# A layered graph kernel: the target column goes through DRAM, and the score addition moves from TensorE and VectorE to GpSimd and ScalarE

## The reference, cut to what matters

```
s, t = h @ u_s, h @ u_t                  # 512-long dot products, one pair per node
e    = leaky_relu(s[:, None] + t[None, :] (+ bias in L2))
e    = where(edge, e, -1e9 or -inf)
out  = softmax(e, axis=-1) @ h           # L0 then applies elu, which changes nothing here
```

## Time and profile before

| | |
|---|---|
| median of 3 runs | 3774.3 us (3770.13 to 3774.59) |
| the profiled execution | 3771.3 us |
| its span, first to last instruction | 3769.4 us |
| granted TensorE clock, mean | 0.986 |
| VectorE, ScalarE, GpSimd busy, share of the span | 82%, 52%, 50% |

### The profile page before, as it was taken

How to read it: one execution, slowest core, us unless ns; L and a number is a source line. 1 busy time by engine, 2 the same in 40 slices (tenths; PEclk the granted TensorE clock), 3 DMA queues, 4 the chain that set the end, 5 groups by cost and what they waited for, 6 DMA issues and landing times.

```text
span 3769.4 us, 75317 instructions
## 1 busy us (share of the span) xinstructions
PE 3567.6 (95%) x25488; PEld 3231.1 (86%) x25488; DVE 3088.7 (82%) x6892; ACT 1949.1 (52%) x4770; POOL 1867.9 (50%) x2852
## 2 busy tenths in 40 slices
PE   3899999999999999999999999999999999999996
PEld 2788888888888888888888888888888888888885
DVE  6788888888888888888888888888888888888874
ACT  2455555555555555555555555555555555555552
POOL 4355455445455545555554554554555545545543
PEclk7999999999999999999999999999999999999997
DMA  3000000000000000000000000000000000000000
GB/s 122 14 20 20 26 20 20 26 20 20 23 23 20 20 26 20 20 26 20 20 26 20 20 26 20 20 26 20 20 26 20 20 26 20 20 23 23 20 16 12
DMA packets 62512, 90.10 MB, mean 24 GB/s; under 512 B 9265, under 2 KB 25777, under 8 KB 62129
## 3 DMA queue, kind: packets, MB, share of 16 engines
q1 hardware_dynamic: 62128, 85.30, 6.9%
HBM read 51.72 MB, written 33.55 MB: 23 GB/s over the span
## 4 chain that ended last, share of the span: by engine, by line
PE 73%; DVE 16%; ACT 5%; issue 4%; POOL 1%; DVEq 0%; ACTq 0%; POOLq 0%
PE bank_c L360 20%; PE bank_b L360 18%; PE bank_e L360 10%; PE bank_e L401 6%; DVE product L805 5%; PE bank_a L368 4%; PE bank_e L380 4%; PE bank_e L335 3%; PE bank_b L335 3%; DVE g L1045 2%; DVE x L831 2%; DVE nlE L1016 2%; DVE nlE L1028 2%; ACT g_hi L740 2%; ACT xa L702 2%
## 5 line engine op out<-in xcount | busy, mean ns | idle before, releaser
L598 ACT ACTIVATE h<-x,rs 128x512 f32<-128x512 f32 x384 | 311.8, 812 | 383.5 <-POOL rs L1114 383.5
L360 PE MATMUL bank_c<-w_hi,g_hi 128*128 128x258 f32 x2048 | 433.2, 293 | 76.4 <-ACT g_hi L740 75.7
L1109 POOL TENSOR_SCALAR rs<-mv 128x1 f32<-128x1 f32 x512 | 142.0, 277 | 688.3 <-DVE mv L798 659.4
L1189 POOL TENSOR_TENSOR nlE<-nlE,nmE 128x512 f32<-128x512 f32 x256 | 265.9, 1038 | 416.1 <-DVE nmE L1036 416.1
L360 PE MATMUL bank_c<-w_lo,g_hi 128*128 128x258 f32 x2048 | 413.3, 283 | 0.0
L360 PE MATMUL bank_b<-w_lo,hT_hi 128*128 128x344 f32 x1536 | 409.3, 321 | 0.0
L360 PE MATMUL bank_b<-w_hi,hT_hi 128*128 128x344 f32 x1536 | 408.7, 320 | 0.0
L360 PEld LDWEIGHTS bank_c<-w_hi,g_hi 128*128 128x128 f32 x2048 | 314.8, 189 | 97.4 <-ACT g_hi L740 96.4
L360 PE MATMUL bank_c<-w_hi,g_lo 128*128 128x258 f32 x2048 | 350.7, 283 | 0.0
L360 PE MATMUL bank_b<-w_hi,hT_lo 128*128 128x344 f32 x1536 | 345.8, 320 | 0.0
L656 ACT ACTIVATE hT_hi<-bank_e 128x512 fp32r<-128x512 f32 x128 | 76.7, 600 | 499.6 <-PE bank_e L352 499.6
(11 more groups left out here) (158 smaller groups left out, 10294.7 us busy)
## 6 DMA issues: line engine op xcount, KB each, us to landing
x_in<-in_x SPq DMA_DIRECT2D x128, 256.0 KB, 2.6
out<-out_sb SPq DMA_DIRECT2D x128, 256.0 KB, 2.0
adj_in<-in_adj SPq DMA_DIRECT2D x128, 64.0 KB, 2.5
pTE<-in_L_gnn_att_src SPq DMA_DIRECT2D x1, 512.0 KB, 4.2
pE<-in_L_gnn_att_dst SPq DMA_DIRECT2D x1, 512.0 KB, 5.1
xl<-in_L_gnn_W SPq DMA_DIRECT2D x1, 512.0 KB, 6.0
x<-in_L_gnn_W SPq DMA_DIRECT2D x2, 256.0 KB, 5.7
out_sb<-in_L_gnn_W SPq DMA_DIRECT2D x2, 256.0 KB, 6.4
```

The lines of the kernel that those rows point to most:

```text
L360: last = mm(bank[:, 0:width], a[:, c * P:(c + 1) * P], w[:, c, b * width:(b + 1) * width], start=(first and c == chunks[0] and n == 0), st ...
L598: activation(h[layer][:, 0, :], src, ACT.Relu, bias=rs[layer][:, 2:3], scale=rs[layer][:, 1:2])\
L1189: tt(nlE[:, half, :], nlE[:, half, :], nm, ALU.subtract).then_inc(sem(f"L3_shifted{i}"), 1)
```

## The change

In L0 and L2 the score matrix is no longer made on TensorE. SP writes the target column to a small DRAM tensor, waits for it, and reads it back spread over all 128 partitions (`spread_targets`). GpSimd subtracts the mask (`masked`). ScalarE adds the source column as its bias and does the leaky step in one instruction (`leaky_one`, function Prelu). VectorE only takes the row maximum (`most`). The waits for a free `bank_a` move from the score steps to `turn_exp_L0` and `turn_exp_L2`. SP's turn becomes load, weights, `spread_targets(2)`, store, `spread_targets(0)`. The sign is no longer turned, so two instructions of the prologue that negated rows go or become copies; the bias of L2 is added as the start value of the sum.

```diff
+            def spread_targets(layer, g):
+                key, s = f"L{layer}", g.slot(2)
+                sp.wait_ge(sem(f"st_made{layer}"), g.made())
+                sp.wait_ge(sem(f"t_spread{layer}"), 16 * g.made(1))
+                sp.dma_start(t_dram[layer][s].rearrange("(n a) -> n a", a=1), st[layer][:, 1:2])\
+                    .then_inc(sem(f"t_sent{layer}"), 16)
+                sp.wait_ge(sem(f"t_sent{layer}"), 16 * g.made())
+                sp.wait_ge(sem(f"{key}_v"), g.made(1))
+                sp.dma_start(t_all[layer][:], t_dram[layer][s:s + 1, :].to_broadcast([P, P]))\
+                    .then_inc(sem(f"t_spread{layer}"), 16)
...
             def turn(t):
                 if t.graph(0).live:
                     load(t.graph(0))
-                if t.graph(6).live:
-                    store(t.graph(6))
                 if t.loop is None and t.step == 0:
                     load_rest()
                 if t.loop is None and t.step in (1, 2, 3):
                     stage_weights(prepared[t.step])
+                if t.graph(4).live:
+                    spread_targets(2, t.graph(4))
+                if t.graph(6).live:
+                    store(t.graph(6))
+                if t.graph(0).live:
+                    spread_targets(0, t.graph(0))
...
-                scores_L0()          # TensorE, between turn_h1 and project_L1b_first
-                scores_L2()          # TensorE, between scores_L1a and turn_h3
...
+            def leaky_one(layer, g):
+                key = f"L{layer}"
+                act.wait_ge(sem(f"{key}_v"), g.made())
+                act.wait_ge(sem(f"{key}_exp"), g.made(1))
+                activation(nl1[key][:], t_masked[layer][:], ACT.Prelu, bias=st[layer][:, 0:1], alpha=SLOPE)\
+                    .then_inc(sem(f"{key}_leaky"), 1)
...
+                leaky_L0()           # ScalarE, between hT_hi_L1a and exp_L0
+                leaky_L2()           # ScalarE, between norm1 and exp_L1a
...
+            def most(key, g):
+                dve.wait_ge(sem(f"{key}_leaky"), g.made())
+                dve.wait_ge(sem(f"{key}_exp"), g.made(1))
+                nc.vector.tensor_reduce(nm1[key][:], nl1[key][:], AX_X, ALU.max, negate=True)\
+                    .then_inc(sem(f"{key}_min"), 1)
...
+                def masked(layer, g, m):
+                    key = f"L{layer}"
+                    pool.wait_ge(sem(f"t_spread{layer}"), 16 * g.made())
+                    pool.wait_ge(sem("masks_made"), g.made())
+                    pool.wait_ge(sem(f"{key}_leaky"), g.made(1))
+                    tt(t_masked[layer][:], t_all[layer][:], m, ALU.subtract).then_inc(sem(f"{key}_v"), 1)
...
+                masked_L0()          # GpSimd, after split_weights(0, 1), ahead of norm_2
+                masked_L2()          # GpSimd, between norm_1 and out_L3
```

More of the change, by code:

```diff
@@ L381, in turn_exp_L3 @@
                             last.then_inc(sem(f"L3_turned{i}"), 1)
[L384 to L392, removed]
                 def product_L3():
@@ L501, in turn_exp_L2 @@
                         pe.wait_ge(sem("L2_exp"), Dg.made())
+                        if A.live:
+                            pe.wait_ge(sem("x1_made"), A.made())
+                        else:
+                            pe.wait_ge(sem("x3_made"), Dg.made(1))
                         nc.tensor.transpose(bank_a[:, 0:P], p1["L2"][:], ident[:]).then_inc(sem("L2_turned"), 1)
@@ L636, in norm2, with leaky_L0, leaky_L2 @@
                         norm(2, Dg, ("L2_out", 1))
+                def leaky_L0():
+                    if A.live:
+                        leaky_one(0, A)
+                def leaky_L2():
+                    if Dg.live:
+                        leaky_one(2, Dg)
                 def exp_L0():
                     if A.live:
-                        exp_one("L0", A)
+                        exp_one("L0", A, 1.0)
                 def hT_hi_L1a():
@@ L798, in stats, with score_columns, softmax_one, least @@
                 nc.vector.bn_aggr(mv[layer][:], bn[layer][:]).then_inc(sem(f"mv_made{layer}"), 1)
-            def score_columns(layer, g, scores):
+            first_of = {0: 0.0, 2: attn_b_all[:]}
+            def score_columns(layer, g):
                 dve.wait_ge(sem(f"h_made{layer}"), g.made())
-                dve.wait_ge(sem(scores), g.made(1))
-                for i, row in enumerate((s_row, t_row)):
-                    last = nc.vector.tensor_tensor_reduce(product[:, layer + i, :], h[layer][:, 0, :], row[layer][:], 1.0, 0.0,
+                dve.wait_ge(sem(f"t_sent{layer}"), 16 * g.made(1))
+                dve.wait_ge(sem(f"L{layer}_leaky"), g.made(1))
+                for i, (row, first) in enumerate(((s_row, first_of[layer]), (t_row, 0.0))):
+                    last = nc.vector.tensor_tensor_reduce(product[:, layer + i, :], h[layer][:, 0, :], row[layer][:], 1.0, first,
                                                           ALU.mult, ALU.add, st[layer][:, i:i + 1])
                 last.then_inc(sem(f"st_made{layer}"), 1)
-            def softmax_one(key, g, bank, ns, bias=None):
+            def softmax_one(key, g, bank, ns):
                 dve.wait_ge(sem(f"{key}_scores"), g.made())
                 dve.wait_ge(sem(f"{key}_exp"), g.made(1))
[L813 to L816, removed]
+                ts(nl1[key][:], bank, ns, None, ALU.add).then_inc(sem(f"{key}_v"), 1)
+                least(key, g)
+            def most(key, g):
[3 more added lines that the diff above has]
+                    .then_inc(sem(f"{key}_min"), 1)
+            def least(key, g):
                 dve.wait_ge(sem(f"{key}_v"), g.made())
@@ L883, in min_L0 @@
                     if A.live:
-                        softmax_one("L0", A, bank_a[:, 0:P], st[0][:, 0:1])
+                        most("L0", A)
                 def result_L3():
@@ L964, in min_L2 @@
                     if Dg.live:
-                        softmax_one("L2", Dg, bank_a[:, 0:P], st[2][:, 0:1], attn_b_all[:])
+                        most("L2", Dg)
                 def recip_L1a():
@@ L1127, in split_weights, with masked_L0, masked_L2 @@
                         last.then_inc(sem("w_split"), 1)
+                def masked(layer, g, m):
[4 more added lines that the diff above has]
+                    tt(t_masked[layer][:], t_all[layer][:], m, ALU.subtract).then_inc(sem(f"{key}_v"), 1)
+                def masked_L0():
+                    if A.live:
+                        masked(0, A, mask[:, A.slot(MR), :])
+                def masked_L2():
+                    if Dg.live:
+                        masked(2, Dg, mask_loop[:, Dg.slot(MR), :])
                 def norm_2():
```

28 lines of the change are left out of this document (11 added, 17 removed).

## The result

The change makes the kernel 26% slower: 4748.5 us (median of 4 runs, 4741.7 to 4753.2) against 3773.9, a ratio of 1.258 with a 95% interval of 1.256 to 1.261. The forecast was 3737. The profiled execution took 4753.2 us; its span is 4751.3, at a mean granted TensorE clock of 0.907 against 0.986 before.

The account below looks back on a forecast made before the run. The chain of a turn was taken as TensorE's list for 20.4 us, then VectorE's queue for 7.2. Saving 122 x (0.16 + 0.24) = 49 us, less 12 for the prologue, gave 3737 us; range 3718 to 3775.

Parts of the forecast that it names:

- The transfers: SP's new writes and reads each turn: 2.0 and 2.6 us to land, 4.8 per trip, hidden for L0 and L2.
- slot of 6.6: Time in L0 from the target column being made to GpSimd's `masked_L0`, leaving 1.8 us to spare.
- the late trip: Rival, chance 0.11: L0's round trip exceeds 6.6 us, delaying GpSimd and ScalarE at the turn's head; +212 us, 3986.
- For L2 there are over 8 us: Claim that L2's write, wait and read have over 8 us before GpSimd needs the row, so stay hidden.
- `scores_L2`: TensorE step ahead of `turn_h3`; removing its 0.33 us gains 0.16 a turn, as `turn_h3` then waits for `out_read`, L896.
- the hitch: Gap in `turn_exp_L3` on TensorE, its second four transposes waiting for `exp3(1)`; goes with an earlier `min_L0`, gaining 0.24 us a turn.
- the wait for `g_hi0`: Sign on TensorE: without `scores_L0` ahead of it, this wait grows from 0.61 to 1.0 us, worth nothing.
- ScalarE and GpSimd in mid-turn: New `masked_L2` (0.42) and `leaky_L2` (0.40) before `exp_L1a`; cost 0 under idle cover, at most 0.3 us.
- that rival: Rival, chance 0.04: Prelu needs its own table, so each leaky step brings two table loads; +256 us, 4030.
- The prologue: First turns: weight loads queue on SP behind the new transfers, costing 12 us in all (7 to 17).

Follow-up runs that it names:

- b2: Changed kernel with the 4-byte write kept and waited for, but a row of `x` spread in place of the row just written: 4512.2 us.
- a1: Changed kernel without the write to DRAM and its wait; a row of `x` is spread instead: 3736.3 us.
- a3: Changed kernel writing 128 pieces of 512 bytes (the identity) in place of the target column, its first row spread: 3740.2 us.
- a4: Changed kernel writing one piece of 512 bytes from one partition (the identity's first row) in place of the column, all waits kept: 3738.0 us.
- b1: Changed kernel writing 128 pieces of 64 bytes (part of the identity) in place of the target column: 3740.5 us.
- d2: As b2 (a row of `x` spread), but the column's 4-byte pieces are written 64 bytes apart: 3739.8 us.
- b4: Changed kernel with only L2 going through DRAM and GpSimd; L0's scores and three VectorE steps as before the change: 4153.9 us.
- c1: Kernel before, scores still from TensorE; in L0 and L2 ScalarE does the leaky step from PSUM, VectorE only the maximum: 3739.7 us, ratio 0.991.
- c2: As c1, also for L1b, with its maximum put between the two products of `columns_L0`: 3648.8 us, ratio 0.967 against the kernel before.
- b3: Changed kernel with eight extra matmuls of 256 columns a turn, results unused, in TensorE's wait for the late exponentials: 4796.7 us.

## Why the prediction was wrong

**The step that failed is "The transfers".** It priced the write at 2.0 and the read at 2.6 us and gave 5.2 as the worst for either. The write takes 7.1 (7.3 in b2), above that bound, and the read back 4.7. The round trip is 11.5 us, not 4.8, in a slot of 6.6. The 2.0 came from a row of 256 KB in long pieces, and "if it were as slow as twice a load" had nothing behind it: no row showed 4-byte pieces, and a bound drawn from transfers of another shape was no bound. Even this bound would have missed the slot, 5.2 + 2.6 + 0.2 = 8.0 us against 6.6, yet the range ended at 3775 and the late trip got 0.11. Shown by a1, a3, a4, b1 and d2, each of which takes the price of the write away and lands at 3736 to 3741.

**"For L2 there are over 8 us"** failed with it. The slot was about right (in a4 8.7 us, from the write at 1922.07 to `masked_L2` at 1930.75), the trip is 12.2 (11.7 in b4), and this half alone costs 385 us. That is also why the rival of the late round trip, though it names the place, came out at 3986. By its own working with the measured trip of L0, 4.9 over the slot and 4.5 of it on the chain, it gives 122 x (4.5 - 0.16) + 12 = +541; with the 385 of L2 measured in b4 that is +926, of 975 measured. That it comes so near is in part luck: the two losses need not add, since GpSimd waits 3.18 us for L2's row in b4 and 2.15 in the kernel after. The rival had the mechanism, sized one trip too short and left the other out.

The Trainium skill, "DMA: Bandwidth & Descriptors" (Anatomy of one DMA and Specifications), was weighed in the prediction on three things: a fixed cost of about 2.0 us, a delay when HBM is the target, and read-modify-write below 512 bytes. The section with the fixed cost is about transfers that GpSimd issues; those here are issued by SP. The runs agree with none of the three as the price here, and though the time came out on the side of its sentence on HBM, it was not for that reason: writes into the same DRAM land in 1.4 us in pieces of 64 bytes, in 1.4 in pieces of 4 bytes set apart, and in 1.5 in pieces of 512. A rule on the size of a piece alone, or on the target alone, does not tell these from the 7.1.

**All other terms held in size**, as a4 shows by its rows above: `scores_L2` (though not what sets `turn_h3`), the hitch, the wait for `g_hi0`, ScalarE and GpSimd in mid-turn at no cost. In the kernel after the mask on GpSimd took 0.43 (forecast 0.42) and the leaky step 0.40, by their groups:

```profile
L605 ACT ACTIVATE nl_L<-t_masked,st 128x128 f32<-128x128 f32 x256 | 102.9, 402 | 932.3 <-POOL t_masked L1160 931.8
...
L1160 POOL TENSOR_TENSOR t_masked<-t_all,mask 128x128 f32<-128x128 f32 x128 | 54.9, 429 | 708.6 <-DMA t_all<-t_dram 708.6
...
L591 ACT ACT_TABLE_LOAD x1 | 1.3, 1283 | 0.7 <-PEq L1268 0.7
```

There is one table load, so that rival is out: the leaky step shares a table with the exponential. (The 2.66 us for a switch, which the prediction cites from the Trainium skill, "ScalarE: Activation LUTs", stand there under What ACT_TABLE_LOAD costs, not under Table sets. No run here has a switch.)

**The prologue** was forecast at 12 us with VectorE's splitting in turn 1 starting at 39 in place of 33.16. With the cheap write of a4 it starts at 39.52:

```profile
39.52 0.69 DVE L880 CUSTOM_DVE_ANT_0 product<-xl,h 128x512 bf16<-128x512 f32 x1 [6.83 <-DMA xl<-in_L_gnn_W]
```

In the kernel after it starts at 47.60, the round trip again. a4 is in step with its steady turn some 13 us later than before, read off the same instruction of VectorE in the same turn, once the turns are steady (188.23 against 174.75).

## What to carry to other kernels

A transfer is priced by a row with pieces of the same size and the same place of landing; where no such row exists, measure it first or keep its range open upwards, for the gain that hangs on it (here 0.4 us a turn) is small beside what is lost when the slot is missed. Before a result is sent through memory and back, follow the loop: who makes the next input of the trip, and does it stand behind what the trip delivers? Two trips in series set the turn, however short the engines' own lists are. And work taken off VectorE pays only where something on the chain waits for it: c1 takes it off twice outside VectorE's own stretch and wins 34 us, nearly all of it the hitch (122 x 0.23 = 28); c2 takes it off once more inside that stretch, and wins 91 on top.

## What the hardware showed that was not expected

- 128 pieces of 4 bytes written side by side into 512 bytes of DRAM: 7.1 to 7.3 us to landing. The same pieces 64 bytes apart: 1.4. 64-byte pieces: 1.4; 512-byte pieces: 1.5. Where between 4 and 64 bytes of distance the cost goes away was not tried, and what makes neighbours wait is open.
- Reading back a row written in this way and spreading it to 128 partitions took 4.7 us; rows written otherwise 3.0 to 3.1; 128 different rows of 512 bytes 1.9. Why the first is slower is open.
- The load of `x`, issued right behind the read, held SP for 2.16 us in the turn shown and landed in 5.0 us at the median, against 2.6 before and 3.4 in b2, where only the row read is another. What couples the two is open.
- After a wait of 3.94 us the granted clock was 0.66 over the next 4.71 us; in b3, with TensorE kept busy through most of the wait, it was 1.00 over the 3.12 us behind it.
